# Rows of the head pieces as (row, head), the head stacks read by one and three transfers, query and key weights in four loads, the values' weights prepared one phase earlier

## The reference

```python
def _L0_attn_ref(x, Wq, bq, Wk, bk, Wv, bv, Wo, bo):
    q = (x @ Wq + bq).reshape(b, s, H, L)
    k = (x @ Wk + bk).reshape(b, s, H, L)
    v = (x @ Wv + bv).reshape(b, s, H, L)
    q = _apply_rope(q, cos, sin)
    k = _apply_rope(k, cos, sin)
    scores = einsum('bnqd,bnkd->bnqk', q, k) / sqrt(L)
    attn = softmax(where(causal, scores, -1e9))
    return einsum('bnqk,bnkd->bnqd', attn, v) ... @ Wo + bo
...
xn = _layernorm(x)
x = x + _L0_attn_ref(xn, ...) + _L0_ffn_ref(xn, ...)
xn = _layernorm(x)
x = x + _L1_attn_ref(xn, ...) + _L1_ffn_ref(xn, ...)
```

## Time and profile before

| what | us |
|---|---|
| median of 3 runs | 1014.62 |
| lowest and highest of them | 1014.4, 1017.1 |
| time of the profiled execution | 1014.82 |
| its span in the trace | 1012.3 |
| busy in the span: PE / DVE / POOL / ACT | 973.6 / 840.8 / 776.1 / 744.4 |

### The profile page before, as it was taken

How to read it: one execution, slowest core, us unless ns; L and a number is a source line. 1 busy time by engine, 2 the same in 40 slices (tenths; PEclk the granted TensorE clock), 3 DMA queues, 4 the chain that set the end, 5 groups by cost and what they waited for, 6 DMA issues and landing times.

```text
span 1012.3 us, 23657 instructions
## 1 busy us (share of the span) xinstructions
PE 973.6 (96%) x7956; PEld 673.0 (66%) x7956; DVE 840.8 (83%) x2259; ACT 744.4 (74%) x1998; POOL 776.1 (77%) x959
## 2 busy tenths in 40 slices
PE   5889999999999999999999999999999999899998
PEld 4556665766666666666666666666666676677776
DVE  7989999788879888877787878877788778989995
ACT  5989987666676677766767676766666776889994
POOL 3777768778777787878787878787877565899995
PEclk9999999999999999999999999999999999999999
DMA  8733445243442333233333333433333200111111
GB/s 261 254 111 118 151 129 153 82 131 106 124 118 86 107 119 95 88 106 111 95 96 115 95 95 96 119 100 102 98 95 96 73 2 16 34 47 35 49 55 43
DMA packets 102902, 101.31 MB, mean 100 GB/s; under 512 B 13952, under 2 KB 98560, under 8 KB 102144
## 3 DMA queue, kind: packets, MB, share of 16 engines
q1 hardware_dynamic: 102784, 99.81, 32.6%
HBM read 56.25 MB, written 40.90 MB: 96 GB/s over the span
## 4 chain that ended last, share of the span: by engine, by line
PE 75%; DVE 10%; POOL 6%; ACT 4%; issue 2%; DMA 2%; SPq 0%; DVEq 0%; POOLq 0%; ACTq 0%
PE bank L1713 24%; PE bank L1810 13%; PE bank L1796 12%; PE bank L1827 8%; PE bank L1784 6%; PE bank L1785 5%; PE bank L2014 3%; PE bank L1954 3%; DVE arena L1410 2%; POOL arena L651 2%; DVE arena L1426 2%; POOL arena L714 2%; ACT arena L919 1%; DMA arena<-in_weights 1%; DVE arena L1388 1%
## 5 line engine op out<-in xcount | busy, mean ns | idle before, releaser
L651 POOL TENSOR_SCALAR arena<-arena,rc 128x128 f32<-128x128 f32 (+3 forms) x512 | 278.2, 562 | 176.5 <-DVE rc L1419 175.5
L919 ACT ACTIVATE arena<-arena,nm 128x256 f32<-128x256 f32 (+3 forms) x512 | 283.4, 554 | 109.0 <-DVE nm L1410 104.3
L1410 DVE CUSTOM_DVE_ANT_0 arena<-bank,mask_rows 128x256 f32<-128x256 f32 (+3 forms) x512 | 232.9, 483 | 88.6 <-PE bank L1785 83.4
L1796 PE MATMUL bank<-ident,arena 128*128 128x128 f32 x1280 | 211.8, 278 | 9.7 <-DVE arena L1426 4.4
L1796 PEld LDWEIGHTS bank<-ident,arena 128*128 128x128 f32 x1280 | 150.0, 141 | 68.6 <-DVE arena L1426 29.2
L1785 PE MATMUL bank<-arena 128*128 128x256 f16 (+3 forms) x512 | 152.9, 299 | 0.0
L1810 PE MATMUL bank<-arena 128*64 128x512 f32 (+3 forms) x1024 | 152.0, 439 | 0.0
L1784 PE MATMUL bank<-arena 128*128 128x256 f16 (+3 forms) x512 | 139.9, 300 | 1.5 <-DMA arena<-scr 1.5
L1810 PEld LDWEIGHTS bank<-arena 128*64 128x64 f32 x1024 | 67.8, 136 | 95.0 <-issue 70.6
L1426 DVE COPY arena<-bank 128x512 f32<-128x512 f32 (+3 forms) x256 | 124.6, 487 | 3.3 <-PE bank L1796 2.9
L927 ACT ACTIVATE arena<-bank 128x512 f32<-128x512 f32 (+3 forms) x256 | 108.6, 424 | 14.9 <-PE bank L1796 14.2
(11 more groups left out here) (192 smaller groups left out, 2176.2 us busy)
## 6 DMA issues: line engine op xcount, KB each, us to landing
arena<-scr SPq DMA_DIRECT2D x320, 128.0 KB, 2.7
scr<-arena SPq DMA_DIRECT2D x256, 128.0 KB, 1.7
arena<-in_weights SPq DMA_DIRECT2D x5, 1024.0 KB, 7.8
x_sb<-in_x SPq DMA_DIRECT2D x8, 512.0 KB, 9.4
out<-x_sb SPq DMA_DIRECT2D x16, 256.0 KB, 2.2
xscr<-arena SPq DMA_DIRECT2D x12, 256.0 KB, 3.2
arena<-wh SPq DMA_DIRECT2D x40, 64.0 KB, 2.0
xsh<-xscr SPq DMA_DIRECT2D x6, 256.0 KB, 3.4
```

Source lines behind the costliest of these rows:

```text
L651: last = pool.tensor_scalar(pr[slot][:, OFF[i]:OFF[i + 1]], pr[slot][:, OFF[i]:OFF[i + 1]], rc[:, slot, i:i + 1], 1.0, ALU.mult, ALU.mult)
L919: act.activation(pr[slot][:, OFF[i]:OFF[i + 1]], pr[slot][:, OFF[i]:OFF[i + 1]], ACT.Exp, scale=-1.0, bias=nm[:, slot, i:i + 1], accum_out ...
L1410: dve.tensor_tensor_reduce(pr[slot][:, OFF[i]:OFF[i + 1]], s_tile[i], mask_rows[:, SQ - P * (i + 1):SQ], -1.0, -MASKED, ALU.add, ALU.min, ...
L1796: last = pe.transpose(banks[5 + h][:, (i - j) * P:(i - j + 1) * P], pr[2 * par + h][:, OFF[i] + j * P:OFF[i] + (j + 1) * P], ident[:])
```

## The change

1. Head pieces. The 128 rows of a piece are ordered (row, head) instead of (head, row): `halves` writes the query and key weights' high and low parts with a step of four columns, the cosine and sine tables are repeated instead of tiled, the biases are loaded to every fourth partition. In `scr` the four heads of one row now lie side by side, and `qs` is read back by one transfer of 128 x 2048 values, `kd` by two of 64 x 2048 and `kz` by one of 64 x 2048, instead of four and six of 32 x 4 x 512. The one read of `qs` waits for all four writes, those of `kd` for the two high ones, that of `kz` for the two low ones.
2. Query and key weights are loaded in four parts (NW = 4) of 0.5 MB, and their maxima are taken part by part, joined by one small reduction.
3. The order of loads: rows of batch 3, the values' weights and rows of batch 4 go ahead of the sixteen bias transfers.
4. DVE makes all low parts of query and key weights, and only then scales the biases and starts with phase 0. The values' maximum moves from ring -4 to ring -5, its scale from ring -2 to ring -3, the low part from ring -1 to ring -2.
5. ACT takes the row statistics in halves (means in one ring, squares in the next) and makes the values' high part in ring -3 instead of -2.
6. PE: the transpose for the values' maximum and the product after it stand a ring earlier, and 24 filling products stand in ring -4 instead of 60.

```diff
@@ -17,6 +17,7 @@
 NO = 12
+NW = 4
 EPS = 1e-5
@@ -400,9 +401,9 @@
                     src = src.rearrange("p kq (c i) -> p kq c i", i=L)[:, :, PAIR[g], e * HL:(e + 1) * HL]
-                    at = (2 * a + e) * P + pp * L
-                    yield src, [w[:, C_QK:C_V].rearrange("p (kq x) -> p kq x", x=8 * L)[:, :, at:at + L]
-                                .rearrange("p kq (s i) -> p kq s i", s=2) for w in (wh, wl)]
+                    at = (2 * a + e) * P
+                    yield src, [w[:, C_QK:C_V].rearrange("p (kq x) -> p kq x", x=8 * L)[:, :, at:at + P]
+                                .rearrange("p kq (i n s) -> p kq n s i", n=2, s=2)[:, :, pp] for w in (wh, wl)]
@@ -452,19 +453,19 @@
             sp.dma_start(vec[:], vec_d).then_inc(vec_loaded, 16)
-            for k in range(KT):
-                half = slice(k * C_V // KT, (k + 1) * C_V // KT)
-                sp.dma_start(wst_qk[:, half], weights_d[:, half]).then_inc(wqk_loaded[k], 16)
+            for w in range(NW):
+                part = slice(w * C_V // NW, (w + 1) * C_V // NW)
+                sp.dma_start(wst_qk[:, part], weights_d[:, part]).then_inc(wqk_loaded[w], 16)
             sp.dma_start(tabraw[:], tab_d).then_inc(tab_loaded, 16)
+            load_rows(3)
+            sp.dma_start(wst_v, weights_d[:, C_V:C_O]).then_inc(wv_loaded, 16)
+            load_rows(4)
             b4 = bqk_d.rearrange("(q p c e r) -> r q p c e", q=NQ, p=2, c=4, e=2)
...
                     for e in range(2):
-                        sp.dma_start(bcol[h * HL:(h + 1) * HL, :, a, e], b4[:, :, h // 2, c, e],
+                        sp.dma_start(bcol[h:P:4, :, a, e], b4[:, :, h // 2, c, e],
                                      allow_slow_non_contiguous=True).then_inc(b_loaded, 16)
-            load_rows(3)
-            load_rows(4)
-            sp.dma_start(wst_v, weights_d[:, C_V:C_O]).then_inc(wv_loaded, 16)
             for b in (1, 5, 2, 6, 7):
@@ -489,39 +490,40 @@
+            def stacked(pieces):
+
+                return pieces.rearrange("c (r h) s -> (c r) h s", h=4)
+
             def move_queries(quad, par):
...
                 f = 2 * quad
-                after(sp, q_in[par], 64 * (quad // 2))
+                after(sp, q_in[par], 16 * (quad // 2))
                 for piece, tile, made_by, sent in ((0, hi_e, hie_done, hie_sent), (1, hi_o, hio_done, hio_sent),
...
                 after(sp, s_done, 12 * (quad - 1))
-                for piece, sent in enumerate((hie_sent, hio_sent, loe_sent, loo_sent)):
+                for sent in (hie_sent, hio_sent, loe_sent, loo_sent):
                     sp.wait_ge(sent, 16 * (f + 1))
-                    sp.dma_start(qs[par][piece * HL:(piece + 1) * HL],
-                                 scr[par, 0, piece].rearrange("(h r) s -> r h s", h=4)).then_inc(q_in[par], 16)
+                sp.dma_start(qs[par], stacked(scr[par, 0])).then_inc(q_in[par], 16)
...
                 f = 2 * quad + 1
-                after(sp, k_in[par], 96 * (quad // 2))
+                after(sp, k_in[par], 48 * (quad // 2))
                 for piece, tile, made_by, sent in ((0, hi_e, hie_done, hie_sent), (1, hi_o, hio_done, hio_sent),
...
                 after(sp, s_done, 12 * (quad - 1))
+                for sent in (hie_sent, hio_sent):
+                    sp.wait_ge(sent, 16 * (f + 1))
+                for rows in (slice(0, L), slice(L, P)):
+                    sp.dma_start(kd[par][rows], stacked(scr[par, 1, 0:2])).then_inc(k_in[par], 16)
                 sp.wait_ge(kz_zero, 2)
-                for piece, sent in enumerate((hie_sent, hio_sent, loe_sent, loo_sent)):
+                for sent in (loe_sent, loo_sent):
                     sp.wait_ge(sent, 16 * (f + 1))
-                    rows = scr[par, 1, piece].rearrange("(h r) s -> r h s", h=4)
-                    at = (piece % 2) * HL
-                    if piece < 2:
-                        sp.dma_start(kd[par][at:at + HL], rows).then_inc(k_in[par], 16)
-                        sp.dma_start(kd[par][L + at:L + at + HL], rows).then_inc(k_in[par], 16)
-                    else:
-                        sp.dma_start(kz[par][at:at + HL], rows).then_inc(k_in[par], 16)
+                sp.dma_start(kz[par][0:L], stacked(scr[par, 1, 2:4])).then_inc(k_in[par], 16)
@@ -865,15 +867,20 @@
                     row_sums(3)
-                    row_sums(4)
-                elif -AHEAD < n < 3 - AHEAD:
-                    row_sums(n + AHEAD + 4)
+                    row_means(4)
+                elif n == 1 - AHEAD:
+                    row_squares(4)
+                    row_means(5)
+                elif n == 2 - AHEAD:
+                    row_squares(5)
+                    act.wait_ge(setup_done, 2)
+                    weights_high(G_V, wv_hi)
+                    row_means(6)
                 elif n == 3 - AHEAD:
+                    row_squares(6)
                     row_means(7)
...
                     act.activation(w8[:], w8st.rearrange("p (k c w) -> p k c w", k=KT, w=2)[:, :, :, 0], ACT.Copy).then_inc(w8_done, 1)
-                    act.wait_ge(setup_done, 2)
-                    weights_high(G_V, wv_hi)
                 elif n in (7, 8):
@@ -1260,37 +1267,38 @@
             inverse_roots(slice(0, 1), 0)
-            for k in range(KT):
-                dve.wait_ge(wqk_loaded[k], 16)
+            for w in range(NW):
+                dve.wait_ge(wqk_loaded[w], 16)
                 for g in (G_Q, G_K):
-                    half = staged(g)[:, k * 8:(k + 1) * 8]
-                    last = dve.tensor_reduce(wqk_max[:, k, g - G_Q:g - G_Q + 1], half, AX.XYZ, ALU.max, apply_absolute_value=True)
+                    part = staged(g)[:, w * 16 // NW:(w + 1) * 16 // NW]
+                    last = dve.tensor_reduce(wqk_max[:, w, g - G_Q:g - G_Q + 1], part, AX.XYZ, ALU.max, apply_absolute_value=True)
             link(dset, last)
-            dve.tensor_tensor(wmax[:, G_Q:G_V], wqk_max[:, 0], wqk_max[:, 1], ALU.max).then_inc(wmax_done, 2)
+            dve.tensor_reduce(wmax[:, G_Q:G_V], wqk_max.rearrange("p w a -> p a w"), AX.X, ALU.max).then_inc(wmax_done, 2)
             over_partitions(2, 0)
...
             columns_low(0, 1)
+            for g in (G_Q, G_K):
+                pairs_low(g, 0)
+                pairs_low(g, 1)
             dve.wait_ge(b_loaded, 16 * 16)
             for g in (G_Q, G_K):
-                dve.tensor_scalar(bcol[:, :, g - G_Q], bcol[:, :, g - G_Q], inv[:, g:g + 1], None, ALU.mult)
-            pairs_low(G_Q, 0)
-            pairs_low(G_Q, 1)
+                last = dve.tensor_scalar(bcol[:, :, g - G_Q], bcol[:, :, g - G_Q], inv[:, g:g + 1], None, ALU.mult)
+            link(dset, last)
...
                 if n == -AHEAD:
-                    pairs_low(G_K, 0)
-                    pairs_low(G_K, 1)
-                elif n == 1 - AHEAD:
                     dve.wait_ge(wv_loaded, 16)
                     weight_maximum(slice(G_V, G_O))
+                elif n == 1 - AHEAD:
                     row_sums(1)
+                    over_partitions(1, 1)
                 elif n == 2 - AHEAD:
-                    over_partitions(1, 1)
+                    weight_scale(slice(G_V, G_O), 1)
                     row_sums(2)
                 elif n == 3 - AHEAD:
-                    weight_scale(slice(G_V, G_O), 1)
+                    weights_low(G_V, (wv_hi, 1), wv_lo)
@@ -1319,9 +1327,7 @@
-                if n == -1:
-                    weights_low(G_V, (wv_hi, 1), wv_lo)
-                elif n == 0:
+                if n == 0:
                     roots(later_tiles, 1, (3,), wo)
@@ -1841,7 +1847,7 @@
-            FILL = (0, 60, 0, 40)
+            FILL = (0, 24, 0, 40)
@@ -1886,10 +1892,11 @@
                 odds(n + AHEAD)
-                if n == 2 - AHEAD:
+                if n == 1 - AHEAD:
                     weight_maxima(slice(G_V, G_O), 1)
+                elif n == 2 - AHEAD:
+                    maxima_down(slice(G_V, G_O), 1)
                 elif n == 3 - AHEAD:
-                    maxima_down(slice(G_V, G_O), 1)
                     fill(30)
@@ -2092,7 +2099,7 @@
     t = np.stack([np.cos(ang.astype(np.float64)).T, np.sin(ang.astype(np.float64)).T], axis=1).astype(np.float32)
-    return np.ascontiguousarray(np.tile(t, (4, 1, 1)))
+    return np.ascontiguousarray(np.repeat(t, 4, axis=0))
```

8 lines of the change are left out of this document (4 added, 4 removed).

## The result

The changed kernel took 1018.67 us (median of 8 runs, 1017.79 to 1023.40), the kernel before, on the same chip, 1014.78 us (8 runs, 1014.28 to 1017.10): a ratio of 1.0037, 95% interval 1.0025 to 1.0049. It is slower by 3.9 us; the predicted range was 1012.4 to 1017.4.

The account below looks back on a forecast made before the run. PE bounds the rings, so only the opening up to the first exponentials moves time: 1014.82 us plus 0.5 (ACT's 0.6, a little taken back) is 1015.3, median 0.2 lower, 1015.1; range 1012.4 to 1017.4.

Parts of the forecast that it names:

- ACT's queue is last, not the stacks: End of the opening: stacks there at about 45.5 us, ACT's first exponential at 47.75, so ACT decides.
- In the rings no one waits for these transfers, so both count nothing: Stack reads in the rings: fewer issues (2.7 us of SP per quad) and the longer bundled read count nothing.
- first exponential: ACT, end of the opening: first exponential at about 48.4 us against 47.75, 0.6 us later.
- 2.1 more than now: Stack read of 512 KB: some 4.8 us, 2.1 more than now, counting only if the rings' cover were gone.
- 0.7 less 0.45: Quad 0: the keys' last read of 256 KB costs 0.7 us over 128 KB, saves about one 0.45 issue.
- The estimate of 3.2 us: The 512 KB stack read by the skill's fixed 2.0 us plus bytes at 436 GB/s, against some 4.8.
- Rival B: High and low parts: four-column step doubles them, phase 0 and all behind it later, 1021 us; chance 0.06.
- I put nothing on it: PE's gap before phase 1's first product, 1.85 to some 2.3 us: no clock cost taken.
- Scale: DVE, opening: four loads make the inverse scale ready 0.7 us earlier, at 16.4 us for 17.08.
- DVE did not wait for the biases: Biases behind 2 MB of other loads: there by 22 to 23 us, needed at about 24.8, cover 2 us.
- terms of phase 0: DVE, opening: phase 0's four terms end at 27.8 us, where it was 25.4, 2.4 us later.
- the keys' chain then ends at 45: Keys in the opening: low parts to 38.2 us, write, wait and 256 KB read to about 45, scores 0.3 to 0.5 earlier.

Follow-up runs that it names:

- e13: e12 with 95 filling products in place of 30 before the first scores; 1018.58 us, ratio 1.0039 to the kernel before.
- e5: e2 with 115 filling products in place of 30 before the first scores; 1015.13 us, ratio 0.9999 to the kernel before.
- e9: The whole change, unaltered, measured and profiled again; 1019.42 us, ratio 1.0042 to the kernel before.
- e12: Kernel before with bundled stack reads, weights laid out by the host (no step of four columns) and biases to every fourth partition; 1018.47 us, ratio 1.0028.
- e16: e12 with the keys' reads in six again, only the queries' read bundled; 1018.21 us, ratio 1.0029 to the kernel before.
- e3: The whole change with query and key weights laid out by the host, so no step of four columns; 1019.39 us, ratio 1.0038 to the kernel before.
- after: The changed kernel's profiled execution, the slowest of its eight; 1023.4 us, 4.7 above their median.
- e1: Kernel before with only the (row, head) order, its step of four columns and the biases' new order, ten reads kept; 1018.91 us, ratio 1.0035.
- e2: The change with old row order and ten reads: four loads, new load order and moved work alone; 1017.88 us, ratio 1.0026 to the kernel before.
- e10: The whole change with 90 filling products in place of 30 before the first scores; 1018.21 us, ratio 1.0034 to the kernel before.
- e4: The whole change with ten reads of 128 KB in place of the bundled ones, step kept; 1017.87 us, ratio 1.0022 to the kernel before.
- e15: e3 with 110 filling products in place of 30 before the first scores; 1018.31 us, ratio 1.0031 to the kernel before.
- e8: Kernel before with less filling on PE (60 to 24 products before phase 1's last terms, 30 to none before first scores); 1016.09 us, ratio 1.0006.
- e7: Kernel before with only the four loads of query and key weights and their maxima in eight; 1015.19 us, ratio 0.9997.
- e14: e7 with 50 filling products in place of 30 before the first scores; 1014.41 us, ratio 0.9997 to the kernel before.
- e17: Kernel before with four loads, 50 filling products, values' low part moved ahead of the first maxima, values' maximum left in place; 1020.51 us, ratio 1.0056.
- e18: Kernel before with 50 filling products in place of 30 before the first scores; 1015.16 us, ratio 1.0007.
- e11: e7 with 33 filling products before the values' first product; 1015.99 us, ratio 0.9997 to the kernel before.

## Why the prediction was wrong

**What failed.** *"So where the opening ends, ACT's queue is last, not the stacks"*, and with it, for the opening, *"In the rings no one waits for these transfers, so both count nothing"*. I asked who is last at the first exponential and found ACT, with the stacks under cover by a microsecond. I did not ask what hangs on the first scores besides it: DVE's chain of maxima, values' low part, terms, maxima, terms, 45.91 to 54.57 with 0.23 us of idle time. On that chain a late stack counts one for one (e13). The change takes the values' low part out of it, and then PE's own queue has no idle time in its place (e5), so it still counts one for one. ACT was as the sum had it: in e9 it comes to its first exponential at 50.63 without a wait, but the values' product did not wait for it. I even had the number ("2.1 more than now") and set it "against two rings of distance", which quad 0 does not have. For quad 0 I took 0.7 less 0.45. Measured: F 3.4 us later in e9 and 2.4 in e12, of which the reads are a part that no run isolates. The landings themselves were nearer: the one read of 512 KB took 3.5 to 4.5 us (e12, e16, e3, e9, after) where the rows gave 4.8, the reads of 256 KB 3.4 to 4.8 where the earlier trace rows had 3.4. The estimate of 3.2 us rests on a fixed part and a rate that the Trainium skill (DMA: Bandwidth & Descriptors, Anatomy of one DMA) gives for transfers issued by GpSimd; SP issues this one, and the trace has more than 3.2.

**Mis-sized.** Rival B, the step, had the right mechanism, the right direction and a chance of 0.06. Its high parts: 9.49 for 5.01 us, 4.5 more for the 4.9 worked out; low parts 774 ns against its turning point of 0.6 us; its time of 1021 is 2 above e1's 1018.9. I had ranked it low for want of a row with such an operand, and the Trainium skill (SBUF — State Buffer, Door 1) leaned the other way: it lets a step that puts two hits into a 16-byte line run at full rate. This trace does not agree, 1404 ns against 707; the measurement decides.

**Wrong.** *"The clock was 1.00 over the whole stage with that gap in it, so I put nothing on it."* The gap that mattered was another: the one before the first scores, which grows with every microsecond that the stack is late. It cost 2.7 us in the order part (e2 to e5) and, by the profiles, 1.1 in the whole change (S of e9 and e10).

**Right.** The rings are PE's and unchanged: 100 us busy of 100. Scale: 16.4 forecast, 16.04 measured. DVE did not wait for the biases. Low parts in a row, terms of phase 0 and the first exponential came within 0.2 us in e2, where the step is away. That the keys' chain then ends at 45 was wrong even there: 46.80.

Of the change's 4.0 us in e9, F has 3.4. The keys' last low part of POOL ends at 40.81 (38.86 before), so 1.95 us are late phases; e4, with ten reads, has 40.92, so the reads are not their cause, and the step less the earlier scale fits. 7.9 us pass from there to the first scores (6.5 before, 6.8 in e4), so by e4 1.2 of the 1.4 are the bundled reads. That is an estimate from single executions: e2 and e5, also with ten reads, need 8.3 and 8.2. S has 0.7: 1.1 for the clock (e10), less 0.3 for the values' low part that left DVE's chain. Open is why the medians of e15 and e5, both at nearly full clock, lie 3.2 us apart when F explains 1.35.

## What to carry to other kernels

Where a transfer's lateness seems covered by one engine's queue, list every engine that hangs on its consumer and find the one with no idle time behind it; that one's slack is the cover. A transfer that bundles pieces waits for the last of them, and so does whatever stands behind it in its queue (the keys' first write was issued at 37.98 in e12, at 36.98 before): merge pieces where nobody waits for them, and not on the first, tight pass. Before you call a part "alone", list everything else in its edit: here the biases came along. If PE's gap at a hand-over grows, put into the sum that what follows may run at half clock, and test it with filling, in a dose that ends before what PE waits for.

## What was not expected of the hardware

- A float16 result (and operand) at a step of four elements: ACT 1404 ns for 707 at 128x512, DVE 774 for 473 at 128x256; e1, with nothing else changed on ACT, has the same 9.49 us for eight.
- The granted clock lay at its lower level for a time about every gap of PE before the first scores from 2.94 us (e4) to 7.80 (after), eight profiles in all. About shorter gaps the profiles differ: it fell with 2.22 before the first scores (e8) and with 2.09 and 2.23 before the values' product (e7, e14), and did not with 2.50 (e1), 2.23 (e13, e17) and 1.89 (before, e18). No run shows what decides between them.
- The first scores of nearly identical kernels lie up to 2.4 us apart (e7, e11, e14), with the keys' last low part made at 37.8 in all three: the queries' writes landed 2.0 to 3.4 us after issue in e7 and 3.1 to 4.6 in the other two.
- Writes that are issued earlier need not land earlier: the queries' four writes issued from 31.21 in the kernel before landed 2.6 to 4.0 us later, those issued from 29.55 in e3 5.3 to 6.2 us later, with a DMA share of 1.12, 1.05 and 0.90 in the three stretches of 2 us from 28 us on.
